# Window attention on one core: transposes in row tiles, projections in column tiles, means subtracted by Pool, and a new order of the copies

## What is computed

```python
h = layernorm(xf) ; windows of 8 x 8 tokens, N = 64, C = 48, 4 heads of 12
qkv = h @ qkv_w.T + qkv_b
q, k, v = (qkv[0] * scale, qkv[1], qkv[2])
attn = softmax(einsum('whnd,whmd->whnm', q, k) + bias)
o = einsum('whnm,whmd->whnd', attn, v) ; o = o @ proj_w.T + proj_b
xf = shortcut + o
m = layernorm(xf) ; xf = xf + gelu(m @ fc1_w.T + fc1_b) @ fc2_w.T + fc2_b
```

## Time and profile before

| | before |
|---|---|
| median of 3 runs | 1891.44 us (1890.6 to 1894.77) |
| profiled execution: time, span | 1900.3 us, 1898.5 us |
| attention, first to last scores | 38.8 to 757.9 us |
| busy over the span: PE, DVE, ACT, POOL | 96%, 82%, 65%, 34% |
| mean granted TensorE clock | 0.992 |

### The profile page before, as it was taken

One profiled execution on the slowest core, in us unless ns is written; L12 is line 12 of the kernel. 1 busy time (PEld: TensorE's weight loads), 2 busy tenths in 40 slices (PEclk: granted clock), 3 DMA queues, 4 the chain that ended last, 5 costly groups with the idle time before them and its releaser, 6 DMA issues.

```text
span 1898.5 us, 75084 instructions
## 1 busy us (share of the span) xinstructions
PE 1830.0 (96%) x29960; PEld 1558.7 (82%) x29960; DVE 1561.5 (82%) x2842; ACT 1243.4 (65%) x2790; POOL 645.1 (34%) x867
## 2 busy tenths in 40 slices
PE   5999999999999999699999899999999999999997
PEld 4888888888888888455555699999999999999997
DVE  4999999999999999566666787777777878777776
ACT  2888888888888887355555566565665656656564
POOL 4333333333333332501210244352533433435340
PEclk9999999999999999799999999999999999999999
DMA  1222222222222222577876363645645455546341
GB/s 66 66 79 73 74 78 74 78 73 74 78 74 78 73 75 69 134 186 162 169 163 150 82 142 81 150 107 114 143 108 118 129 100 136 112 119 134 91 134 35
DMA packets 286412, 198.46 MB, mean 105 GB/s; under 512 B 225991, under 2 KB 275672, under 8 KB 276504
## 3 DMA queue, kind: packets, MB, share of 16 engines
q1 hardware_dynamic: 282114, 189.12, 39.6%
q0 software_dynamic: 2368, 6.25, 2.0%
q10 hardware_dynamic: 1750, 0.39, 0.1%
HBM read 128.36 MB, written 54.72 MB: 96 GB/s over the span
## 4 chain that ended last, share of the span: by engine, by line
PE 55%; DMA 2%; issue 1%; ACT 1%; DVE 1%; SPq 0%; ACTq 0%; DVEq 0%
PE psum L1124 15%; PE psum L1143 13%; PE psum L1178 9%; PE psum L680 5%; PE psum L1167 5%; PE psum L661 3%; PE psum L651 3%; PE psum L666 2%; DMA room<-tok_mid 1%; DMA room<-in_ident 0%; ACT room L750 0%; DVE room L885 0%; DVE room L712 0%; DVE room L1279 0%; ACT L750 0%
## 5 line engine op out<-in xcount | busy, mean ns | idle before, releaser
L934 POOL TENSOR_TENSOR mats<-mats,dscale 112x2048 f32<-112x2048 f32 x72 | 260.8, 3622 | 270.4 <-DMA mats<-in_taps 268.2
L884 ACT ACTIVATE room<-psum 64x512 f32<-64x512 f32 (+1 forms) x336 | 177.6, 529 | 254.3 <-PE psum L1143 249.1
L1124 PE MATMUL psum<-ew,xp 64*100 64x96 f32 x6144 | 313.8, 251 | 7.3 <-issue 5.9
L1124 PEld LDWEIGHTS psum<-ew,xp 64*100 64x100 f32 x6144 | 290.3, 165 | 13.6 <-issue 9.8
L885 DVE TENSOR_SCALAR h<-psum 100x384 f32<-100x384 f32 x384 | 209.5, 556 | 69.7 <-PE psum L1124 46.6
L885 DVE TENSOR_SCALAR room<-psum 64x512 f32<-64x512 f32 (+1 forms) x336 | 207.6, 618 | 68.9 <-PE psum L1143 62.2
L1143 PE MATMUL psum<-h,mats 101*64 101x128 f32 x4608 | 260.6, 273 | 0.7 <-DVE h L885 0.7
L1143 PEld LDWEIGHTS psum<-h,mats 101*64 101x64 f32 x4608 | 252.9, 137 | 5.2 <-issue 1.1
L344 PE MATMUL psum<-kb,qa 128*64 128x256 f32 x2048 | 244.6, 381 | 0.8 <-DVE prob L443 0.8
L884 ACT ACTIVATE h<-psum 100x384 f32<-100x384 f32 x384 | 188.1, 490 | 58.8 <-PE psum L1124 42.2
L344 PEld LDWEIGHTS psum<-kb,qa 128*64 128x64 f32 x2048 | 140.7, 138 | 56.4 <-issue 2.1
(11 more groups left out here) (158 smaller groups left out, 3411.9 us busy)
## 6 DMA issues: line engine op xcount, KB each, us to landing
mats<-in_taps SPq DMA_DIRECT2D x69, 896.0 KB, 6.2
tok_mid<-mid SPq DMA_DIRECT2D x128, 224.0 KB, 1.9
room<-tok_mid SPq DMA_DIRECT2D x64, 448.0 KB, 4.8
piece<-img_mid SPq DMA_DIRECT2D x196, 63.8 KB, 2.4
img_mid<-room SPq DMA_DIRECT2D x128, 97.5 KB, 3.6
kb<-kk SPq DMA_DIRECT2D x512, 24.0 KB
out<-yc SPq DMA_DIRECT2D x32, 384.0 KB, 4.6
scratch<-in_x_tokens SPq DMA_DIRECT2D x126, 96.0 KB, 2.0
```

Of the source, the lines that this page charges most:

```text
L884: return nc.scalar.activation(dst, src, ACT.Relu)
L934: nc.gpsimd.tensor_tensor(m, m, bc(scale[0:MROWS, at:at + TCH], 2, POUT), ALU.mult).then_inc(mats_scaled, 1)
L1124: mm = nc.tensor.matmul(psum[0:PIN, bank_of(j + u), p:4 * CH:4], xp[hx][rows, 2 * j + p, :], w1[rows, c, :], start=True, stop=True)
```

## The change

Nothing outside `attention` is edited but for the layout of the projection's weights.

- Transposes of `on`, `xn` and the probabilities: instead of a transpose of 128x128, one for each window of 64 rows, with its 64x64 part of the identity, in two row tiles, each into a PSUM bank of its own. The first of each set is an ordinary matmul with the identity.
- y is made by window in column tiles; v in column tiles by head parity, so that two copies of 64x192 replace four of 64x96.
- PE's order in a step: `on`, `xn`, probabilities, q and k (all in row tiles), then y, v, o, and all eight scores of i+1 (all in column tiles).
- q is no longer copied to `qa` by DVE: ACT copies q and k together into `qk`, and SP puts q into `qa` by a fifth transfer behind the four of k.
- The means: DVE keeps the sums, POOL multiplies them by 1/48 (`mean`, `mean2`) and subtracts (`cen`, `cen2`).
- ACT's order: `xnT`, `oT`, both halves of `probT`, q and k (after `qk_ready` and `v_ready`), `lnv`, `rstd`, exp of i, v of i+1. DVE's order: `top`, `prob`, `sqs`, `sums`, `mid`, `sums2`, `rden`, `on`.
- PSUM banks 4 to 7 are laid out anew; `on` has 16 columns a head.

The core of the diff:

```diff
 # SP
                 if has(i + 2):
-                    sp.wait_ge(k_copied, i + 3)
+                    sp.wait_ge(qk_copied, i + 3)
                     for h in range(NH):
                         r = slice(ONE + HD * h, ONE + HD * h + HD)
-                        sp.dma_start(kb[s][r, :, h, :], kk[s][r, :].rearrange("q (n m) -> q n m", m=NT))\
-                            .then_inc(keys_put[s], 16)
+                        sp.dma_start(kb[s][r, :, h, :], qk[s][r, :].rearrange("q (n m) -> q n m", m=NT))\
+                            .then_inc(heads_put[s], 16)
+                    sp.dma_start(qa[s][ONE:ONE + C, :], qk[s][0:C, :]).then_inc(heads_put[s], 16)
 # PE
+            def turn(out, rows, r, first):
+                if first:
+                    return nc.tensor.matmul(out, rows, ident[r, r], start=True, stop=True)
+                return nc.tensor.transpose(out, rows, ident[r, r])
-                        mm = nc.tensor.transpose(ps_p[:, k, at:at + P], prob[1 - s][:, NH * p + 2 * h:NH * p + 2 * h + 2, :],
-                                                 ident[:, :])
+                        for w in range(2):
+                            r = slice(NT * w, NT * w + NT)
+                            mm = turn(ps_p[:, w, at:at + NT], prob[s][r, NH * p + 2 * h:NH * p + 2 * h + 2, :], r, at == w == 0)
-                        mm = nc.tensor.matmul(ps_y[:, 2 * C * a:2 * C * a + 2 * C], oT[:, P * a:P * a + P], w_o[:, :],
-                                              start=True, stop=True)
+                        for w in range(2):
+                            mm = nc.tensor.matmul(ps_y[NT * w:NT * w + NT, 2 * C * a:2 * C * a + 2 * C],
+                                                  oT[:, P * a + NT * w:P * a + NT * w + NT], w_o[:, :], start=True, stop=True)
+                            for h in range(2):
+                                mm = nc.tensor.matmul(ps_v[NT * h:NT * h + NT, at:at + 2 * HD * NH // 2],
+                                                      xnT[1 - s][:, P * a + NT * w:P * a + NT * w + NT], v_part(h),
+                                                      start=True, stop=True)
 # DVE
-                    nc.vector.scalar_tensor_tensor(cen[s][:, :, :], bc(sums[s][:, :], 2, C), -1.0 / C, x_of(i + 4),
-                                                   ALU.mult, ALU.add).then_inc(cen_done, 1)
-                    nc.vector.tensor_copy(halves(qa[s][ONE:ONE + C, :]), ps_k[0:C, :, :].rearrange("q e (a t) -> q e a t", t=P))\
-                        .then_inc(q_copied, 1)
 # ACT, new order
                 if has(i + 2):
                     act.wait_ge(qk_ready, i + 3)
+                    if has(i + 1):
+                        act.wait_ge(v_ready, i + 2)
                     if has(i):
-                        act.wait_ge(keys_put[s], keys_of(i, s))
+                        act.wait_ge(heads_put[s], heads_of(i, s))
+                    nc.scalar.activation(halves(qk[s][0:ONE + C, :]),
+                                         ps_k[0:ONE + C, :, :].rearrange("q e (a t) -> q e a t", t=P), ACT.Copy)\
+                        .then_inc(qk_copied, 1)
                 if has(i + 3) or has(i - 3):
                     act.wait_ge(sqs_done, i + 4)
                     nc.scalar.activation(lnv[:, :], sq_sums[:, :], ACT.Ln, bias=eps[:, :], scale=1.0 / C).then_inc(ln_done, 1)
                     ...
                     nc.scalar.activation(rstd[:, :], lnv[:, :], ACT.Exp, scale=-0.5).then_inc(rstd_done, 1)
 # POOL
+                    pool.wait_ge(sum_done, i + 5)
+                    nc.gpsimd.tensor_tensor(mean[:, :], sums[s][:, :], per_c[:, :], ALU.mult).then_inc(mean_done, 1)
+                    pool.wait_ge(mean_done, i + 5)
+                    nc.gpsimd.tensor_tensor(cen[s][:, :, :], x_of(i + 4), bc(mean[:, :], 2, C), ALU.subtract).then_inc(cen_done, 1)
```

More of the change, by code:

```diff
@@ L43 @@
 VE = HD + 1
+HEAD = 16
 MID = 112
@@ L357, in step @@
                     pe.wait_ge(xn_done, i + 3)
[L358 to L359 removed]
                     for a in range(PAIRS // 2):
[L361 removed]
+                        for w in range(2):
+                            r = slice(NT * w, NT * w + NT)
+                            mm = turn(ps_xT[:, w, NT * a:NT * a + NT], xn[s][r, 2 * a:2 * a + 2, :], r, a == w == 0)
                     mm.then_inc(xnT_ready, 1)
@@ L386, in step @@
                     mm.then_inc(qk_ready, 1)
-                elif has(i):
+                elif has(i + 1):
                     pe.wait_ge(v_copied, i + 1)
+                if has(i - 2):
+                    pe.wait_ge(oT_copied, i - 1)
+                    wait(pe, qk_copied, min(i + 2, GROUPS) if isinstance(i, int) else i + 2)
+                    wait(pe, res_done, i - 2)
+                    for a in range(PAIRS // 2):
+                        for w in range(2):
+                            mm = nc.tensor.matmul(ps_y[NT * w:NT * w + NT, 2 * C * a:2 * C * a + 2 * C],
+                                                  oT[:, P * a + NT * w:P * a + NT * w + NT], w_o[:, :], start=True, stop=True)
+                    mm.then_inc(y_ready, 1)
@@ L398, in step @@
                     mm.then_inc(o_ready, 1)
[L399 to L406, removed]
@@ L413, in step @@
             def step(i, s):
[L414 to L421, removed]
-                    dve.wait_ge(rden_done, i - 1)
-                    nc.vector.tensor_tensor(on[:, :, 0:C].rearrange("q p (h e) -> q p h e", h=NH), o[:, :, :, 0:HD],
-                                            bc(rden[:, :].rearrange("q (p h) -> q p h", h=NH), 3, HD), ALU.mult)\
-                        .then_inc(on_done, 1)
+                sc = ps_s[:, :, :].rearrange("q b (h m) -> q (b h) m", m=NT)
+                if has(i):
+                    dve.wait_ge(s_ready, i + 1)
+                    nc.vector.tensor_reduce(top[s][:, :], sc, AX_X, ALU.max).then_inc(top_done, 1)
+                    dve.wait_ge(top_done, i + 1)
+                    nc.vector.tensor_tensor(prob[s][:, :, :], sc, bc(top[s][:, :], 2, NT), ALU.subtract)\
+                        .then_inc(sub_done, 1)
                 if has(i + 3) or has(i - 3):
@@ L468, in step @@
             def step(i, s):
-                def turned_probs(k):
-                    act.wait_ge(pT_ready, 2 * i - 1 + k)
-                    nc.scalar.activation(probT[:, 2 * k:2 * k + 2, :, :].rearrange("q p h n -> q (p h n)"), ps_p[:, k, :], ACT.Copy)\
-                        .then_inc(pT_copied, 1)
-                if has(i):
-                    act.wait_ge(v_ready, i + 1)
-                    v = ps_v.rearrange("q (b h e) -> q b h e", h=2, e=HD)
-                    for h in range(2):
-                        for w in range(2):
-                            dst = vb[s][NT * h:NT * h + NT, :, :, w, VE * h:VE * h + HD].rearrange("q p k e -> q (p k) e")
-                            last = nc.scalar.activation(dst, v[NT * w:NT * w + NT, :, h, :], ACT.Copy)
-                    last.then_inc(v_copied, 1)
+                if has(i + 2):
+                    act.wait_ge(xnT_ready, i + 3)
+                    nc.scalar.activation(by_window(xnT[s][:, :]), turned_by_window(ps_xT), ACT.Copy).then_inc(xnT_copied, 1)
@@ L511, in step @@
                     nc.scalar.activation(prob[s][:, :, :], prob[s][:, :, :], ACT.Exp).then_inc(exp_done, 1)
+                if has(i + 1):
+                    act.wait_ge(v_ready, i + 2)
+                    if has(i - 1):
+                        act.wait_ge(o_ready, i)
+                    for h in range(2):
+                        r = slice(NT * h, NT * h + NT)
+                        last = nc.scalar.activation(
+                            vb[1 - s][r, :, :, :, VE * h:VE * h + HD].rearrange("q p k w e -> q w (p k) e"),
+                            ps_v[r, :].rearrange("q (w x e) -> q w x e", w=2, e=HD), ACT.Copy)
+                    last.then_inc(v_copied, 1)
             schedule(act, step, lambda act: put_bias(act, lambda dst, src: nc.scalar.activation(dst, src, ACT.Copy), 1), -1)
@@ L1310, in placed_taps, with placed_projection @@
     return placed
+def placed_projection(w, b):
+    rows = np.zeros((NH, HEAD, C), np.float32)
+    rows[:, 0:HD] = w.T.reshape(NH, HD, C)
+    rows[0, HD] = b
+    return rows.reshape(NH * HEAD, C)
 def kernel(**inputs):
```

157 lines of the change are left out of this document (80 added, 77 removed).

## The result

The changed kernel takes 2067.78 us (median of 4 runs, 2064.82 to 2071.16) against 1893.11 us for the kernel before on the same chips: ratio 1.0893, 95% interval 1.0868 to 1.0917. It is slower, as forecast, but by 175 us where 100 were forecast, and it lies outside the stated range of 1955 to 2028. The profiled execution took 2066.82 us with a span of 2065.0 us.

The account below looks back on a forecast made before the run. PE was taken to bound the kernel before, at 5.64 us a step. Afterwards a 12.94 us round trip over two steps gives 6.47: 123 x 0.83 = +102, less 2, so 1991 us (2000 on the profile's own time); range 1955 to 2028.

Parts of the forecast that it names:

- The chain named in the prediction: Round trip of q and k, from scores to scores two steps on: 12.94 us, 6.47 a step against 5.64.
- The gate (step 2 of the change of order): SP's puts wait for `lnv`, `rstd`, POOL's `xn` and `mid`, then the store: 1.83 of 2.88 us growth.
- scores to transposes: On PE, from the start of scores to the next step's first transpose: 1.83 plus 0.05, 1.88 us.
- ACT's pick-up and copy: ACT takes up v's last result 0.13 later and copies q and k in 0.59: 0.72 us.
- to the last result of v: 2.70: On PE, from the first transpose through q and k, y and v until v's last result: 2.70 us.
- three of them are ordinary matmuls of two passes ... I take 0.05: Three of PE's 24 row-tiled transposes cost extra; 0.05 was taken, giving 0.82 us for the set.
- q and k start at 1.05: On PE, q and k wait for ACT's copy of `xnT`, ended at 1.00, and start at 1.05 instead of 0.82.
- q's put until it lands: 1.97: SP's fifth put takes 1.97 us from issue to landing; high end 2.4, with an issue of 0.8 instead of 0.35.
- The high ends that the prediction named: Transposes, q's put and late wake-ups add 0.9 us: 6.92 a step, 2046 us; range stopped at two thirds.
- the clock at 1.00: PE keeps full granted clock in attention; the rival, 0.75, gave 7.1 us a step, 2069 us, 5 in 100.
- PE alone would go round in 5.3: PE's work of 5.06 us plus its wait for `xnT` makes a step of 5.3 us.
- The rival that said 1847 us: PE sets the pace, all trips hidden, 5.3 us a step: 44 us faster, 1847 us; 2 in 100.

Follow-up runs that it names:

- experiment 1: The changed kernel with SP's five puts placed ahead of the store of `mid`: 1940.6 us, ratio 1.0187 to the kernel before.
- experiment 3: The changed kernel with the puts ahead of the store of `mid` and q put by ACT: 1914 us, ratio 1.0058 to the kernel before.
- experiment 4: The changed kernel with POOL writing `mid` ahead of `xn`: 2044 us, ratio 1.0728 to the kernel before.
- experiment 12: The changed kernel with `lnv` and `rstd` ahead of ACT's copy of q and k again: 2029 us, ratio 1.0689 to the kernel before.
- experiment 2: The changed kernel with q put from ACT's queue right behind the copy, SP's store still first: 2091 us, ratio 1.0994 to the kernel before.
- experiment 7: The changed kernel with the 128x128 transposes of before and the copies that go with them: ratio 1.0912 to the kernel before.
- experiment 9: The changed kernel with puts ahead of the store, q put by ACT, and PE also waiting for `xn` before transposing `on`: ratio 1.0063 to the kernel before.
- experiment 11: The kernel before with y made in column tiles behind q and k, nothing else: 1887.2 us, ratio 0.9925.

## Why the prediction was right and wrong

**Right: the cause.** The chain named in the prediction is the one that the trace shows, term for term, and experiments 1, 3, 4 and 12 move it by about what it says. The gate (step 2 of the change of order) is most of it: 7 of the 9 points go with the place of one store (experiment 1). Of its terms, scores to transposes (1.87 for 1.88), ACT's pick-up and copy (0.73 for 0.72), `lnv` and `rstd` (0.50 for 0.48), POOL (1.13 for 1.10), `mid` to the first put (0.65 for 0.64) and the four puts (3.40 for 3.37) held.

**Wrong: the size.** The trip is 13.76 and not 12.94. Two terms make 0.73 of the 0.82, and the six above add the other 0.09:
- "to the last result of v: 2.70": it is 3.16, and this is the step that failed first. "three of them are ordinary matmuls of two passes ... I take 0.05": it is 0.16 on top of a transpose, so the copy of `xnT` ends at 1.21 instead of 1.00. And "q and k start at 1.05" takes PE to go on 0.05 behind that copy. In every second step, the one that is in this trip, it is 0.32, with three register operations in PE's queue; the sum had nothing for them. Together q and k start at 1.53.
- "q's put until it lands: 1.97", and 0.08 for PE: 2.32 from issue to scores. Its issue takes 0.58, between the plain 0.35 and the 0.8 of a key put that I named as the high end.

The 0.82 us are 0.41 a step, 52 us in 127 steps. The high ends that the prediction named, 0.9 us more and so 13.84, would have covered the trip; the range stopped at two thirds of them. Even the full 2046 us would have fallen short of 2068, because of the clock.

**Wrong: the clock at 1.00.** I gave the clock a chance of 5 in 100 and a price of 180 us. The total of 2068 lies beside that rival's 2069, but by accident: the granted clock is 0.97, not 0.75, over 200 to 300 us. It falls to 0.5, that is 1.2 GHz, for 6.8 us seven times in attention (one fall is in the last two windows above). Two overlapping trips hold each fall, of 16.2 to 16.6 us instead of 13.76. Three trips one behind the other around a fall take 43.7 us instead of 41.3, so a fall costs 2.4 and all seven some 17 us. The row that I used, 12.42 busy of 15 at clock 1.00, has PE pause for 0.76 us at the longest. The steady stretch has pauses of 2.3 us, because one of two steps takes the whole wait; the prediction had it spread evenly, 1.1 in each.

The other traces point the same way. Where PE pauses for 2.3 us every second step (experiment 2) the granted clock over 100 to 700 us is 0.95 (the changed kernel's is 0.98), with pauses of 1.8 (experiment 4) 0.97, of 1.4 (experiment 12) 0.99, and without long ones (experiments 1 and 3) 1.00. Experiment 7 tells most: its trip is as long as the changed kernel's, but there the wait drifts from uneven to even and back, and around 380 us both of two steps wait for about 1 us. Its clock doesn't fall between 106 and 591 us.

```profile
340.00:420.00 80.00, 68.70 (x1091) 54.57 (x1092) 51.50 (x95) 50.31 (x118) 38.12 (x92) 1.00 0.25 75
```

But pauses of up to 2.1 us stand there without a fall as well, and 7 has other transposes. So the link between long pauses and falls is argued from these rows, not isolated.

Adding up for attention: trip 1.23 x 127 = 156, clock 17, start and end about -5 (the first seven steps take 43.6 us instead of 48.2): 168.

**Wrong without effect on the forecast: "PE alone would go round in 5.3".** Even with all transfers out of the way the changed order runs at 5.75. The rival that said 1847 us couldn't have come: ACT's time, "costed at nothing", is part of a loop of 5.75 us.

## What to carry to other kernels

An in-order queue turns a wait into a wait for everything behind it: when a producer moves on one engine, look on every queue at what stands behind the waits for its result, transfers above all. Follow such a chain around to where it starts, over as many steps as it spans, and compare it with the steps' pace; busy shares show neither it nor a loop of short pieces on an engine that is 74% busy. A gain on an engine counts only up to the next loop: 0.16 us less of transposes on PE gave nothing (experiment 9). And the time from one start to the next holds more than the work: y's 0.52 us held 0.10 of a change of division, which stayed when y became cheaper, so that 0.16 us less gave 0.06 (experiment 11).

## What the runs showed of the hardware that was not expected

- A matmul of 64x128 by 64x64 in float32, in a row tile, holds it for about 0.22 us, and the same as a transpose for 0.06. With three such matmuls among the 24 of a step, the row-tiled part takes 1.27 us where 12 full transposes took 1.31 (12 x 0.109).
- The change from full transposes to row tiles costs 0.10 us on PE: eight transposes last 0.97 until the next start with it and 0.87 without (experiment 11 against the kernel before).
- Three register operations in PE's queue come with 0.27 us more ahead of q and k (gap 0.32 against 0.06).
- A transfer of 48 rows of 2 KB between two SBUF tiles takes 0.58 us to issue on SP and 0.52 on ACT; ACT's next instruction starts 0.66 behind the end of the one ahead of it.
- A trip over two steps with too little slack sets the time of two steps and not how they share it: in the changed kernel one waits 2.3 us and the other nothing, in experiment 7 the shares drift, and around 380 us both wait for about 1 us.
- PE, busy 83 of 100 us with pauses of 2.3 us every 13.8, lost full clock seven times in 887 us, each time for 6.8 us. In the kernel before, with pauses of 0.76 us at the longest in a stretch of the MLP, it kept it.
